# Flamingo block, experts' loop: order of weight subtractions, token products and selection

## What is computed

```
x = x + tanh(g_xattn) * attention(layernorm(x), ctx)      # 16 heads, 8 x 1500 keys
x = x + tanh(g_ffn)   * experts(layernorm(x))

experts(h):  combine = top-2 of softmax(h @ gate_w.T), normalised      # 8 experts
             gate, up = split(h @ gate_up_w[e].T)                      # 512 each
             out = sum over e of combine[:, e] * ((up * gelu(gate)) @ down_w[e].T)
```

## Time and profile before

| | us |
|---|---|
| median of 3 runs | 299.88 (297.85 to 300.0) |
| the profiled execution | 299.23 |
| its span, first to last instruction | 297.5 |

### The profile page before, as it was taken

How to read it: one execution, slowest core, us unless ns; L and a number is a source line. 1 busy time by engine, 2 the same in 40 slices (tenths; PEclk the granted TensorE clock), 3 DMA queues, 4 the chain that set the end, 5 groups by cost and what they waited for, 6 DMA issues and landing times.

```text
span 297.5 us, 8034 instructions
## 1 busy us (share of the span) xinstructions
PE 284.7 (96%) x2826; PEld 218.9 (74%) x2826; DVE 220.0 (74%) x420; ACT 181.3 (61%) x370; POOL 102.5 (34%) x113
## 2 busy tenths in 40 slices
PE   7988999999999999999999999999889998998994
PEld 3464867876886886786787688887688887887862
DVE  4688878678786786777867878677256988888861
ACT  1635677676667757766767666557528775666500
POOL 4598423114015113312311411024500464776300
PEclk9999999999999999999999999999999999999999
DMA  7397960991792595298097079600000000000001
GB/s 249 88 203 196 220 194 16 209 249 54 162 264 96 103 218 197 52 220 248 0 218 198 0 156 240 237 0 2 2 2 0 1 2 0 0 1 0 0 0 31
DMA packets 9924, 32.19 MB, mean 108 GB/s; under 512 B 2576, under 2 KB 3088, under 8 KB 9904
## 3 DMA queue, kind: packets, MB, share of 16 engines
q1 hardware_dynamic: 9472, 31.60, 41.9%
q10 hardware_dynamic: 432, 0.33, 0.3%
HBM read 13.26 MB, written 0.23 MB: 45 GB/s over the span
## 4 chain that ended last, share of the span: by engine, by line
PE 86%; DVE 7%; issue 3%; ACT 2%; DMA 1%; SPq 0%; DVEq 0%; POOL 0%; ACTq 0%
PE score_ps L927 17%; PE max_ps L947 14%; PE o_ps L961 14%; PE misc_ps L915 7%; PE misc_ps L909 5%; PE score_ps L1190 3%; PE score_ps L1191 3%; PE score_ps L1192 3%; PE max_ps L977 3%; PE o_ps L1272 2%; PE misc_ps L999 2%; DVE part_max L687 2%; PE score_ps L909 2%; PE max_ps L970 1%; PE misc_ps L1106 1%
## 5 line engine op out<-in xcount | busy, mean ns | idle before, releaser
L687 DVE TENSOR_REDUCE part_max<-max_ps 112x1 f32<-112x512 f32 (+1 forms) x192 | 118.5, 670 | 40.4 <-PE max_ps L947 38.2
L510 ACT ACTIVATE probs<-score_ps 128x448 f32<-128x448 f32 x192 | 92.0, 543 | 28.9 <-PE score_ps L927 27.2
L947 PE MATMUL max_ps<-kx,qx 96*112 96x512 f32 (+1 forms) x192 | 77.5, 410 | 2.0 <-DVE part_max L687 0.9
L927 PEld LDWEIGHTS score_ps<-qx,kx 104*128 104x128 f32 (+1 forms) x384 | 66.5, 187 | 15.0 <-issue 7.9
L927 PE MATMUL score_ps<-qx,kx 104*128 104x224 f32 (+1 forms) x384 | 76.9, 285 | 0.5 <-ACT probs L510 0.4
L362 POOL TENSOR_TENSOR k_low<-k_full,k_high 128x512 fp32r<-128x512 f32 (+1 forms) x21 | 26.3, 1256 | 67.6 <-ACT k_full L493 67.3
L961 PE MATMUL o_ps<-probs,v_sb 128*32 128x112 f32 (+1 forms) x1536 | 47.6, 262 | 1.0 <-ACT probs L510 1.0
L961 PEld LDWEIGHTS o_ps<-probs,v_sb 128*32 128x32 f32 (+1 forms) x1536 | 36.1, 109 | 13.2 <-ACT probs L510 6.1
L947 PEld LDWEIGHTS max_ps<-kx,qx 96*112 96x112 f32 x192 | 33.8, 177 | 6.6 <-issue 2.9
L422 POOL TENSOR_TENSOR kx<-gu_sb,kx 128x512 fp32r<-128x512 f32 x16 | 23.0, 1440 | 30.6 <-ACT kx L590 30.4
L505 ACT ACTIVATE v_sb<-misc_ps 128x512 f32<-128x512 f32 x24 | 14.4, 601 | 20.0 <-PE misc_ps L915 20.0
(11 more groups left out here) (177 smaller groups left out, 376.7 us busy)
## 6 DMA issues: line engine op xcount, KB each, us to landing
kx<-k_high SPq DMA_DIRECT2D x60, 187.5 KB, 3.9
kx<-k_low SPq DMA_DIRECT2D x30, 187.5 KB, 3.9
ctx_sb<-in_ctxT SPq DMA_DIRECT2D x7, 750.0 KB, 6.1
gu_sb<-in_guT SPq DMA_DIRECT2D x8, 512.0 KB, 4.7
dn_sb<-in_dnT SPq DMA_DIRECT2D x8, 256.0 KB, 5.1
ctx_sb<-in_ctxT SPq DMA_DIRECT2D x2, 256.0 KB, 4.1
kx<-k_high SPq DMA_DIRECT2D x4, 123.5 KB, 2.3
kx<-k_high SPq DMA_DIRECT2D x4, 64.0 KB, 2.0
```

The costliest lines, as they stand in the source:

```text
L510: nc.scalar.activation(probs[:, (KT * h + t) % 8, :], score_ps[:, t % 3, 0:SC // 2], ACT.Exp, scale=SCALE).then_inc(exp_done, 1)
L687: nc.vector.reduce_max(part_max[:, p, c:c + 1], max_ps[0:PC, bank, 0:size], AX.X).then_inc(max_taken, turns)
L927: last = nc.tensor.matmul(score_ps[0:m, t % 3, GC * g:GC * g + GC], kx[0:KR, 2 * par + h, g, 128 * t:128 * t + m], qx[0:KR, par, 2 * h + g ...
L947: nc.tensor.matmul(max_ps[0:PC, bank, 0:size], qx[0:MR, par, 2 * h + p // 2, PC * (p % 2):PC * (p % 2) + PC], kx[0:MR, slot, p // 2, start ...
```

## The change

ScalarE copies UP and GATE one expert further ahead, at the end of an expert's work (UP(1) and GATE(3) in front of the loop), and DOWN(e+1) at its start, after a wait for the first up product; gelus 0 and 1 stand behind high part 2, gelus 2 and 3 behind high part 3. GpSimd waits for the expert's tokens (`xe_ready`) instead of its first up product, selects, subtracts UP and GATE, then waits for the second low part of hact (`hact_ready`) and subtracts DOWN. VectorE does three products before the first remainder, and the cast of the next tokens behind the last. TensorE does two gates and the spread before the first down product, and the last two downs together.

```diff
--- before.py
+++ after.py
@@ -452,18 +452,19 @@
             weights_rest(GATE, 2, 0, 5)
 
             def expert(i, par):
+
                 e = batch(i, par)
-                pool.wait_ge(up_done, FT * e + 1)
+                pool.wait_ge(xe_ready, e + 1)
                 select(e + 1, 1 - par)
-                made = 3 * e + 5
-                weights_rest(UP, e + 1, 1 - par, made + 1)
-                weights_rest(DOWN, e + 1, 1 - par, made + 2)
-                weights_rest(GATE, e + 3, 1 - par, made + 3)
+                weights_rest(UP, e + 1, 1 - par, 3 * e + 6)
+                weights_rest(GATE, e + 3, 1 - par, 3 * e + 7)
+                pool.wait_ge(hact_ready, FT * e + 2)
+                weights_rest(DOWN, e + 1, 1 - par, 3 * e + 8)
 
             def last_expert(i, par):
 
                 e = batch(i, par)
-                pool.wait_ge(up_done, FT * e + 1)
+                pool.wait_ge(xe_ready, e + 1)
                 select(e + 1, 1 - par)
                 weights_rest(UP, e + 1, 1 - par, e + 16)
 
@@ -609,32 +610,35 @@
             act.wait_ge(combT_done, 1)
             nc.scalar.activation(combT, max_ps[0:16, 1, 0:TOK], ACT.Copy).then_inc(combT_saved, 1)
 
-            def expert(i, par, split_gate=True):
+            def expert(i, par, split_down=True, split_gate=True):
                 e = batch(i, par)
 
-                def next_gelu(j):
-                    gelu(e + 2, par, j)
-
-                for j in range(FT):
+                def hact_copy(j):
                     act.wait_ge(hact_full, FT * e + j + 1)
                     nc.scalar.activation(hact_parts[:, j, 0, :], hact[:, j, :], ACT.Copy).then_inc(hact_high, 1)
-                    if j == 1:
-                        next_gelu(0)
-                weights_copy(UP, e + 1, 1 - par)
-                next_gelu(1)
+
+                if split_down:
+                    act.wait_ge(up_done, FT * e + 1)
+                    weights_copy(DOWN, e + 1, 1 - par)
+                hact_copy(0)
+                hact_copy(1)
+                hact_copy(2)
+                gelu(e + 2, par, 0)
+                gelu(e + 2, par, 1)
+                hact_copy(3)
+                gelu(e + 2, par, 2)
+                gelu(e + 2, par, 3)
+                weights_copy(UP, e + 2, par)
                 if split_gate:
-                    weights_copy(DOWN, e + 1, 1 - par)
-                next_gelu(2)
-                if split_gate:
-                    weights_copy(GATE, e + 3, 1 - par)
-                next_gelu(3)
-
+                    weights_copy(GATE, e + 4, par)
+
+            weights_copy(UP, 1, 1)
+            weights_copy(GATE, 3, 1)
             with act.Fori(0, 2) as i:
                 expert(i, 0)
                 expert(i, 1)
-            expert(2, 0)
-            expert(2, 1, split_gate=False)
-            weights_copy(UP, E - 1, 1)
+            expert(2, 0, split_gate=False)
+            expert(2, 1, split_down=False, split_gate=False)
             act.wait_ge(down_done, E * FT)
             nc.scalar.activation(yT, o_ps[:, 0:TOK], ACT.Copy).then_inc(y_saved, 1)
 
@@ -866,14 +870,14 @@
 
                 product(0)
                 product(1)
+                product(2)
                 rest(0)
-                product(2)
                 rest(1)
                 product(3)
                 x_expert_full(e + 1, 1 - par)
                 rest(2)
+                rest(3)
                 x_expert_copy(e + 1, 1 - par)
-                rest(3)
                 x_expert_rest(e + 1, 1 - par)
 
             with dve.Fori(0, E // 2 - 1) as i:
@@ -1256,11 +1260,15 @@
                 for j in range(FT):
                     up(e, par, j)
                 pe.wait_ge(weights_low, 3 * e + 5)
-                for j in range(FT):
-                    next_gate(j)
-                    down(j)
-                    if j == 0:
-                        spread_weight(e + 1, 1 - par)
+                next_gate(0)
+                next_gate(1)
+                spread_weight(e + 1, 1 - par)
+                down(0)
+                next_gate(2)
+                down(1)
+                next_gate(3)
+                down(2)
+                down(3)
 
             with pe.Fori(0, E // 2 - 1) as i:
                 expert(i, 0)
```

## The result

| | before | changed |
|---|---|---|
| median, 18 runs each | 298.64 (297.45 to 301.56) | 297.12 (296.02 to 298.95) |
| the profiled execution | 299.23 | 297.22 |
| its span | 297.5 | 295.5 |
| from its start to U(0) | 229.80 | 230.43 |
| U(0) to U(6) | 51.03 | 48.44 |

The ratio is 0.9937, 95% interval 0.9913 to 0.996: 0.6% less, about 1.9 us by the ratio and 1.5 by the two medians, within one per cent. In the profiled executions the experts' stage gave 2.59 us, and 0.63 of it was lost ahead of the stage, where the change has no instruction.

What follows compares the result with a forecast made beforehand. TensorE, busy 96%, was taken as the bound, idling when VectorE is held behind GpSimd. Expert 0 ending at 238.25 plus 5 x 8.0 gives 278.25 against 280.83, 2.6 less: 297.3 us, range 295.3 to 299.7.

Steps and rivals of the forecast that it cites:

- Total: Whole kernel: 2.6 us less, 297.3 from the runs' median of 299.88 and 296.6 for the profiled execution.
- Stage: From expert 0's first up matmul, U(0), to expert 6's, U(6): 2.6 us less than 51.03.
- The step on the first expert: Expert 0, first up matmul to expert 1's: next start at 238.25 instead of 237.78, a loss of 0.47 us.
- The pace: TensorE's time per expert after the first: 8.0 us, between 7.9 and 8.1, five times in the sum.
- The bad experts: Kernel before: VectorE late in every second expert, two remainders held 1.1 us each, about 0.9 becoming idle TensorE.
- The steady expert: Experts after the first: remainder 0 waits 0.1 at most, remainder 2 is partly held by DOWN, tokens ready at 7.3 us.
- First rival: Every expert keeps the first one's pattern, GATE's subtraction holding remainder 1: pace 8.45, 299.6 us; chance 0.15.
- Second rival: A VectorE remainder touching a GpSimd subtraction pays a fixed 1.73 us, however short the touch: pace 9.4, 306.2 us; chance 0.05.
- Third: TensorE's own pace exceeds 8.1 through waits for gelus in the new order: worth -1 us, near 299; chance 0.08.
- The step that was off: Carrying the profiled stage's whole 2.6 us gain over to the runs' median: 299.88 - 2.6 = 297.3.

Runs made afterwards that it cites:

- the small subtractions: GpSimd subtracts 8 of 512 columns from expert 1's weights on: in the kernel before 296.4 us (0.9931), in the changed kernel 295.6 us (0.9908).

## Why the prediction came out as it did

- **Total.** 297.3 was forecast and 297.12 measured, 296.6 forecast for the profiled execution and 297.22 measured; the latter misses 0.6, all of it ahead of U(0), where I had assumed the same clock. That the median fits so closely is partly luck: I took 2.6 from 299.88, the median of three runs, and 18 runs of before have 298.64. The gain is 1.5 by the medians and 1.9 by the ratio, for 2.6 forecast.
- **Stage.** 2.6 was forecast (51.03 to 48.4) and 2.59 measured, but with two errors that cancel by luck, about 0.35 us each. The step on the first expert said 8.45, it is 8.80: it took remainder 0 to go first once UP(1) had ended, and it was held for GATE(3) as well. The pace said 8.0, and it is 7.91 from expert 2 on; the lower end of my 7.9 to 8.1 was right, since expert 2 of before contained delays of its own.
- **The bad experts.** I wrote that VectorE is late "in every second expert". The steps show two of six, experts 1 and 4. The sum doesn't use it.
- **The steady expert.** In expert 1 remainder 0 is held 0.1 (it takes 0.68), remainder 2 until DOWN's end plus 0.48 (1.05 long; I had 0.8), the tokens are ready 7.5 after U (246.72 - 239.23; I had 7.3), and gates and downs have no wait: the mechanism is the forecast one, the holds a little longer. Two premises can be seen apart: TensorE's pace without holds is 7.91 with the small subtractions, and the three products of expert 1 take 0.62 each beside GpSimd's two subtractions, which take 2.56 together.
- **First rival** (every expert like the first): no; but the thin margin of which it spoke is real. With GpSimd released 1 us later the steps are 8.5.
- **Second rival** (a fixed 1.73 per touch): no, by 0.68 and 1.05. What is left of the GpSimd instruction is paid. The Trainium skill, page "SBUF — State Buffer", "Who interferes with whom", calls the contention of the two an exclusive lock, from which this follows. By that rule the trace now agrees, with 0.68 and 1.05, where the earlier trace rows couldn't tell. The row of 2.04 shows the case that I hadn't priced, being held by more than one.
- **Third** (gelus late): TensorE waited for none.
- **The step that was off** is the last, from the profiled execution to the median. I took 51.0 as the stage of every execution of before. One in five profiles has 49.8, and the times at full clock suggest, without showing it, that it is more than half of the executions: the changed kernel's 296.02 to 296.73 lie about 2.4 under the five slower executions of before, and about 1.3 under the eight faster ones. Where one hold falls away by chance, the kernel before has already won 1.2 of what the change makes certain. So the two intervals (1.2 to 2.6 us by the first ratio, 0.6 to 2.1 by the second) don't reach beyond 2.6. The changed kernel has 48.44 and 48.45 in its two profiles.

## What to carry to other kernels

Where VectorE's instructions with two SBUF inputs and GpSimd's meet, order the work so that GpSimd runs under VectorE's reads from PSUM, and give it a wait that holds it there; releasing it 1 us later cost 2.0 us here, and dropping its wait ahead of DOWN 3.6, of which about 1.6 went by TensorE's clock. Look in the trace for meetings within 0.05 us: they fall either way from execution to execution, and a sum made from one profile counts them as certain. Before moving an instruction on one engine, follow what stands behind it on the next two: the old TensorE order cost 6.7 us with ScalarE's new one (up to 1.6 of it by the clock), though TensorE's longest single wait was 1.5.

## What was not expected of the hardware

A waiting VectorE remainder isn't always the next one in. It was held by two subtractions in a row in the changed kernel (2.04 us) and by three when DOWN followed at once (3.79 us for two remainders), in each case where it arrived 0.3 us before the end of the first; arriving 0.04 after a start or 0.16 before an end, it had the next turn. And TensorE's granted clock fell to 0.79 and 0.57 over 8 us, at 28 to 36 us, in some executions of the same program and not in others, which moved U(0) by up to 3 us. It also fell to 0.50 in expert 0 of the two kernels in which TensorE had stood idle for 1.74 and 1.49 us there, at about 1.6 us a time.
